# Attention block on one core: units by halves of the sequence, a 512-column output projection, 512-wide value jobs

## What is computed

```
x = x + 0.5 * FFN(layernorm(x))      # FFN: layernorm, ternary 256x256 weight, bias
x = x + ATTN(layernorm(x))           # 16 query heads, 4 key/value heads, head size 128
x = x + 0.5 * FFN(layernorm(x))
# ATTN: q, k, v projections + bias; rotary on q and k; key j is seen by query i
# when 0 <= i - j <= 64; softmax; weights @ v; concatenated heads @ Wo + bo
```

## Time and profile before

| | us |
|---|---|
| median of 3 runs (791.47, 792.79, 792.71) | 792.71 |
| span of the profiled execution, first to last instruction | 790.5 |
| PE busy / PEld busy | 778.3 / 727.2 |
| DVE / ACT / POOL busy | 626.1 / 469.6 / 455.7 |
| mean granted clock of PE, share of full | 0.998 |

### The profile page before, as it was taken

How to read it: one execution, slowest core, us unless ns; L and a number is a source line. 1 busy time by engine, 2 the same in 40 slices (tenths; PEclk the granted TensorE clock), 3 DMA queues, 4 the chain that set the end, 5 groups by cost and what they waited for, 6 DMA issues and landing times.

```text
span 790.5 us, 16087 instructions
## 1 busy us (share of the span) xinstructions
PE 778.3 (98%) x5630; PEld 727.2 (92%) x5630; DVE 626.1 (79%) x1321; ACT 469.6 (59%) x1602; POOL 455.7 (58%) x466
## 2 busy tenths in 40 slices
PE   8999999999999999999999999999999999999997
PEld 7688999999999999999999999999999999999996
DVE  5888967988688877888769887688867988688757
ACT  5366665657646565655747556475664657645574
POOL 3778555766446754567536773476635676446443
PEclk9999999999999999999999999999999999999999
DMA  8572324352252423425153242533224452243410
GB/s 300 114 194 59 90 55 120 95 127 48 55 152 63 121 54 89 126 55 120 41 135 94 68 99 49 134 92 97 67 55 121 94 129 45 57 104 68 107 29 27
DMA packets 54352, 74.10 MB, mean 94 GB/s; under 512 B 7168, under 2 KB 30208, under 8 KB 54272
## 3 DMA queue, kind: packets, MB, share of 16 engines
q1 hardware_dynamic: 53712, 72.74, 37.7%
q10 hardware_dynamic: 560, 0.34, 0.2%
HBM read 14.33 MB, written 4.19 MB: 23 GB/s over the span
## 4 chain that ended last, share of the span: by engine, by line
PE 92%; DVE 3%; POOL 2%; DMA 1%; issue 1%; ACT 0%; SPq 0%; DVEq 0%; POOLq 0%
PE job_p L656 33%; PE attn_p L656 22%; PE scores_p L673 13%; PE heads_p L656 11%; PE probsT_p L737 7%; PE job_p L833 4%; PE job_p L817 2%; POOL q_s L1282 1%; DMA x_res<-wo 1%; POOL probs L1271 1%; DMA x_in<-x 0%; DVE parts L1015 0%; DMA rope_swap<-rope_sin 0%; POOL wo_s L1253 0%; DVE rope_sin L934 0%
## 5 line engine op out<-in xcount | busy, mean ns | idle before, releaser
L656 PE MATMUL attn_p<-wo_s,headsT 128*128 128x256 f32 x1536 | 209.2, 286 | 1.0 <-ACT headsT L1175 0.7
L656 PE MATMUL job_p<-xnT,wq_s 128*128 128x512 f32 x768 | 205.3, 403 | 1.2 <-DVE v_s L951 1.1
L656 PEld LDWEIGHTS attn_p<-wo_s,headsT 128*128 128x128 f32 x1536 | 196.5, 191 | 7.0 <-ACT headsT L1175 1.4
L1154 ACT ACTIVATE probs<-scores_p,neg_max 128x96 f32<-128x96 f32 x512 | 167.6, 352 | 51.8 <-DVE neg_max L900 51.6
L1271 POOL TENSOR_TENSOR probs<-probs,inv_sum 128x384 f32<-128x384 f32 x128 | 107.9, 843 | 152.0 <-DVE inv_sum L906 151.9
L1282 POOL TENSOR_TENSOR q_s<-q_s,rope_swap 128x512 f32<-128x512 f32 x128 | 164.3, 1291 | 52.3 <-DMA rope_swap<-rope_sin 52.2
L1175 ACT ACTIVATE headsT<-heads_p,columns_s 128x512 fp32r<-128x512 f32 x128 | 88.0, 688 | 140.9 <-PE heads_p L656 140.5
L656 PEld LDWEIGHTS job_p<-xnT,wq_s 128*128 128x128 f32 x768 | 135.8, 189 | 26.6 <-DVE v_s L951 1.7
L934 DVE SCALAR_TENSOR_TENSOR rope_sin<-job_p,columns_s,rope_t 128x512 f32<-128x512 f32 x160 | 118.9, 743 | 21.1 <-PE job_p L656 19.9
L673 PE MATMUL scores_p<-k_s,q_s 128*128 128x96 f32 (+2 forms) x1024 | 131.6, 272 | 0.3 <-POOL q_s L1282 0.2
L673 PEld LDWEIGHTS scores_p<-k_s,q_s 128*128 128x128 f32 x1024 | 126.5, 192 | 3.4 <-POOL q_s L1282 1.1
(11 more groups left out here) (96 smaller groups left out, 972.7 us busy)
## 6 DMA issues: line engine op xcount, KB each, us to landing
rope_swap<-rope_sin SPq DMA_DIRECT2D x320, 128.0 KB, 2.3
v_odd<-v_s SPq DMA_DIRECT2D x64, 192.0 KB, 3.3
x_in<-x SPq DMA_DIRECT2D x15, 256.0 KB, 4.2
out<-x_res SPq DMA_DIRECT2D x15, 256.0 KB, 2.5
x_tr<-x_transposed SPq DMA_DIRECT2D x7, 512.0 KB, 5.3
q_s<-wq SPq DMA_DIRECT2D x3, 512.0 KB, 10.1
q_s<-wo SPq DMA_DIRECT2D x2, 512.0 KB, 10.6
x_res<-wo SPq DMA_DIRECT2D x2, 512.0 KB, 4.8
```

Of the source, the lines that this page charges most:

```text
L656: mm = nc.tensor.matmul(dst, a(p), b(q), start=clears and i == 0, stop=len(pairs) == 1, skip_group_check=True)
L1154: ins = nc.scalar.activation(probs[:, i, k, 0:REACH], scores_p[i][:, k, 0:REACH], ACT.Exp, bias=neg_max[:, i, k:k + 1], accum_out=row_sum[ ...
```

## The change

1. `group_block`: units run by halves of the sequence. Units 0 to 7 are groups 0 to 3 with blocks 0 and 1, units 8 to 15 groups 0 to 3 with blocks 2 and 3 (last batch: the last four units by block, groups 2 and 3). A group's `q_s`, `k_s` are free after unit 8 + 2g + 1 (`freed`).
2. `project`: `attn_p` is one tile of two banks; the bank is that of block t % 2, in strips of 256 columns. For each head one matmul of 512 columns (high heads x [high | low] Wo) writes both strips, and one of 256 columns (low x high) adds to strip 0: eight matmuls for twelve, except in the last two units of the last batch.
3. `after_attention` adds both strips: two DVE ops where one was, with a semaphore between them. Both halves use the same two banks.
4. `value_job`: one block of 128 tokens, all 512 value columns: six matmuls of 512 columns; still four jobs a batch. `shift_values`: three shifts a batch, two DMAs each.
5. Banks: the 14 jobs between the prologue's and the first T use four banks, the two of `attn_p` beside `job_p`.
6. `residual` on POOL in halves; one more wait in `exp_of`, in `statistics` and a changed one in `scores`.
7. All five lists are rewritten. K and Q: K0 to K2 and Q0 to Q8 of the next batch are made in the current one (before: K0, Q0 to Q3). In the first batch all 20 K and Q jobs come before unit 6's scores (before: three K and eleven Q). The second FFN of half 0 (YT2_0, FO2_0) comes in its own batch.

Core of the diff:

```diff
 def group_block(x):
     i, b = x[1:]
-    if b < BATCHES - 1 or i < UNITS // 2:
-        return divmod(i, BLOCKS)
-    g, t = divmod(i - UNITS // 2, 2) if i < UNITS - NKV else divmod(i - UNITS + NKV, 2)[::-1]
-    return NKV // 2 + g, t if i < UNITS - NKV else t + BLOCKS // 2
+    g, t = divmod(i % (UNITS // 2), 2)
+    if b == BATCHES - 1 and i >= UNITS - NKV:
+        g, t = NKV // 2 + i % 2, (i - UNITS + NKV) // 2
+    return g, t + (BLOCKS // 2 if i >= UNITS // 2 else 0)
+def freed(g):
+    return UNITS // 2 + 2 * (g + 1)
...
+PROLOGUE_JOBS = 6
+EARLY_JOBS = len(numbered(PE_STEPS[:PE_STEPS.index(("T", 0, 0))], *(x[0] for x in JOB_LIST)))
+BANKS = [n % 2 if n < PROLOGUE_JOBS else (n - PROLOGUE_JOBS) % 4 if n < EARLY_JOBS else (n - EARLY_JOBS) % 2
+         for n in range(len(JOBS))]
...
                 for h in range(GROUP):
-                    products(*head(h), LEFT_HIGH, opens and h == 0)
+                    heads, n = head(h)
+                    if last_pair(x):
+                        products(bank[:, 0, :], heads, lambda s: wo_s[:, s, n, :], LEFT_HIGH, g == NKV // 2 and h == 0)
+                    else:
+                        nc.tensor.matmul(bank, heads(0), wo_s[:, :, n, :], start=g == 0 and h == 0, stop=False,
+                                         skip_group_check=True)
                 pe.wait_ge(heads_lo, u + 1)
                 for h in range(GROUP):
-                    mm = products(*head(h), LEFT_LOW)
+                    heads, n = head(h)
+                    mm = products(bank[:, 0, :], heads, lambda s: wo_s[:, s, n, :], LEFT_LOW)
...
+                if m < 3:
+                    add(blocks, attn_p[:, banks, 1, :]).then_inc(attn_added, 1)
+                    dve.wait_ge(attn_added, 2 * b + m + 1)
+                add(blocks, attn_p[:, banks, 0, :]).then_inc(attn_read, 1)
...
 TENSOR "first"
-        K1c Q4c Q5c S0c S1c Q6c V10c T0c Q7c W0c T1c S2c S3c O0c
+        V0c K0c Q0c Q1c Q2c Q3c Q4c K1c Q5c Q6c Q7c S0c Q8c Q9c V1c S1c T0c Q10c K2c W0c Q11c S2c S3c T1c V2c Q12c
+        O0c Q13c W1c S4c T2c O1c K3c W2c S5c T3c Q14c Q15c O2c W3c T4c FO1_0n O3c W4c T5c S6c S7c O4c V3c W5c T6c
 TENSOR "middle", units 6 to 9
-        W5c T6c Q13c S8c O5c FO0n W6c T7c S9c Q14c FO1n O6c W7c T8c Q15c S10c O7c W8c XT0n T9c
+        T6c S8c XT_0n O5c W6c S9c XT_1n V0n T7c O6c W7c K0n O7c Q0n T8c Q1n W8c Q2n S10c T9c O8c V1n
 VECTOR "middle", the same place
+        heads6c XT_1n V0n probsT7c inv9c heads7c K0n evac0c Q0n probsT8c Q1n stats2_0c heads8c Q2n
 TENSOR "last", its end
-        T14c YT0c O13c W14c T15c O14c YT2c W15c FO0c O15c YT3c FO2c FO3c
+        T14c O13c W14c T15c FO2_0c O14c W15c YT3_2c O15c YT3_3c FO3_2c FO3_3c
 GPSIMD "first", its begin
-        w7f probs0c probs1c K1c Q4c Q5c Q6c Q7c probs2c w9f K2c scale0n probs3c w10f
+        w6f w3f pad0f w8f w10f K0c Q0c Q1c Q2c Q3c Q4c w7f K1c Q5c probs0c Q6c Q7c Q8c Q9c probs1c scale1_0n Q10c
```

More of the change, by code:

```diff
@@ L95 @@
+    "epilogue": "",
 }
@@ L216 @@
 PARTS = {"p": -1, "c": 0, "n": 1}
-WAVES = ("YT", "FO", "stats", "scale", "norm", "bias")
 def program(table):
@@ L225, in program @@
         for step in (table[name] if name in table else table["middle"]).split():
-            kind = step[:-1].rstrip("0123456789")
-            index, part = step[len(kind):-1], step[-1]
+            kind, index = step[:-1].split("_") if "_" in step else (step[:-1].rstrip("0123456789"), None)
+            index, part = index or step[len(kind):-1], step[-1]
             at = b + PARTS[part] if part in PARTS else {"i": -1, "f": 0}[part]
@@ L370, in block_kernel @@
         job_p = [psum(f"job_p{i}", [P, SEQ]) for i in range(2)]
-        attn_p = [psum(f"attn_p{i}", [P, 2, E]) for i in range(2)]
+        attn_p = psum("attn_p", [P, 2, 2, E])
         consts_in = sem("consts_in")
@@ L378, in block_kernel @@
         x_loaded = [sem(f"x_loaded{m}") for m in range(2)]
-        out_stored = sem("out_stored")
+        out_stored = [sem(f"out_stored{m}") for m in range(2)]
         staged = [sem(f"staged{i}") for i in range(10)]
@@ L383, in block_kernel @@
         split_lo_pool = sem("split_lo_pool")
-        v_shifted = sem("v_shifted")
+        v_shifted = [sem(f"v_shifted{m}") for m in range(BLOCKS - 1)]
         ones_set = sem("ones_set")
@@ L662, in scores @@
                 if t == 0:
-                    pe.wait_ge(rope_added, ROPED["Q", GROUP * g + GROUP - 1, b] + 1)
+                    pe.wait_ge(rope_added, max([ROPED["K", g, b]] + [ROPED["Q", GROUP * g + h, b] for h in range(GROUP)]) + 1)
                 pe.wait_ge(mask_ready, u + 1)
@@ L754, in wait_for_bank, with wait_for_sums @@
                     pe.wait_ge(ffn_added, FFN_OUT[was] + 1)
+            def wait_for_bank(x):
+                n = JOBS[x]
+                before = [i for i in range(n) if BANKS[i] == BANKS[n]]
+                if before:
+                    wait_for_job(JOB_LIST[before[-1]])
+                elif BANKS[n] > 1:
+                    wait_for_sums(BANKS[n] - 2)
+            def wait_for_sums(i):
+                if i:
+                    pe.wait_ge(gamma_copied, 1)
+                else:
+                    pe.wait_ge(bias_ready, 1)
+                    if FIRST_BIASED:
+                        pe.wait_ge(first_biased, len(FIRST_BIASED))
             def rope_job(x):
@@ L848, in beta_product @@
                 pe.wait_ge(rows_in, 16)
-                nc.tensor.matmul(attn_p[0][:, 0, :], identf[:, :], half_b, start=True, stop=False)
+                nc.tensor.matmul(attn_p[:, 0, 0, :], identf[:, :], half_b, start=True, stop=False)
                 pe.wait_ge(columns_in, 16)
@@ L1013, in statistics @@
                 half = blocks_of(x)
+                before = [i for y, i in NORMED.items() if i < n and blocks_of(y).start < half.stop and half.start < blocks_of(y).stop]
+                if before:
+                    dve.wait_ge(rstd_ready, 2 * before[-1] + 2)
                 for at in range(half.start, half.stop):
```

333 lines of the change are left out of this document (150 added, 183 removed).

## The result

The changed kernel takes 802.89 us (median of four runs, 800.94 to 804.09) against 792.75 for the kernel before (791.47 to 793.4): ratio 1.0132, 95% interval 1.0111 to 1.0152. It is slower by 10 us where 7.4 of gain were forecast. The profiled execution spans 800.2 us, against 790.5.

What follows compares the result with a forecast made beforehand. PE's own sequence was taken as the bound, busy all 660 us from 80 to 740. Merges -5.8, T/S order -1.2, start -1.9, middle stalls +1.5 gave -7.4 us: median 785.3, range 780.5 to 790.5.

Steps and rivals of the forecast that it cites:

- Merges (part 2 and 4): PE's O and V jobs: 696 merges of two 256-column matmuls into one of 512, 0.0083 us each, 5.8 us gained.
- Order of T and S (part 7): PE's list: scores directly ahead of a transposition 49 times instead of 9, 0.03 us each, 1.2 us gained.
- Middle batches: Shorter T-to-W queue distances on PE: 0.25 us lost a batch, 1.5 in six; bounds 0 and 7.
- Rival (4): Middle batches: stalls of about 1.2 us a batch eat all the gain, 792 us; chance 0.05.
- The held op: Middle batches: narrow DVE op held at ports shared with POOL; 1.2 us in full every batch gave the bound of 7.
- Start: Up to unit 6's scores, put at 74.5 us: net 1.9 us gained; bounds 5 gained and 2 lost.
- Rival (2): Start gains nothing or loses 2 us, POOL and DVE bounding until the last rope job; 787.2 to 789; chance 0.12.
- Four banks: Start's early jobs: four banks absorb the 0.1 to 0.3 us each job loses waiting for DVE with two.
- Rival (1): Middle batch: DVE becomes the bound at evac0, adding both strips; slower, 802 us; chance 0.09.
- The end: Last ops are the same chain with the same lengths, PE still the bound: nothing, between -1 and +1.5 us.

Runs made afterwards that it cites:

- experiment 1: Changed kernel with the 696 merged 512-column matmuls of O and V split back into 256-column pairs: 807.17 us, ratio 1.0189 to the kernel before.
- experiment 9: Changed kernel with XT_0, XT_1 and V0 later on PE in middle batches, ACT's and DVE's lists following: 821.71 us, ratio 1.0374 to the kernel before.
- experiment 12: Changed kernel with POOL's 512-wide residual moved behind the next batch's scale step in middle batches: 805.54 us, ratio 1.0159 to the kernel before.
- experiment 10: Changed kernel with the edits of experiments 4, 5, 6 and 7, plus DVE's heads 5 ahead of the second half's statistics: 805.36 us, ratio 1.0139.
- Experiment 5: Changed kernel with the shift DMAs behind Q6 in SP's list, first and middle batches: 801.23 us, ratio 1.0115 to the kernel before.
- experiment 7: Changed kernel with POOL's first-batch FFN steps behind Q15's add, DVE's and PE's FFN steps later accordingly: 806.12 us, ratio 1.0156 to the kernel before.
- experiment 8: As experiment 7, but unit 6's and 7's probabilities and maxima ahead of most of the moved steps: 807.43 us, ratio 1.0184 to the kernel before.
- experiment 6: Changed kernel with split w3 ahead of w6 on POOL at the very start: 802.56 us, ratio 1.0106 to the kernel before.
- experiment 3: Changed kernel with two job banks throughout, not four for the early jobs: 807.38 us, ratio 1.0173 to the kernel before.
- experiment 2: Changed kernel with DVE's adds of the second strip left out, result incomplete: 803.51 us, ratio 1.0133 to the kernel before.
- experiment 4: Changed kernel with heads 5 and probsT 6 first on ACT, O5 ahead of XT_0 on PE, middle batches: 801.55 us, ratio 1.0117 to the kernel before.
- experiment 13: Changed kernel with the edits of experiments 4, 5, 6 and 12 together: 800.64 us, ratio 1.0092 to the kernel before.
- experiment 14: Changed kernel with the edits of experiments 5, 6 and 12 together: 798.45 us, ratio 1.0082 to the kernel before.

## Why the prediction was wrong

**Merges (part 2 and 4): right, and too small.** Forecast 5.8, measured 7.4 to 8.3 in PE's sequence (experiment 1), though only 4.5 in the time. I took 0.232 for a 512 and 0.120 for a 256 from jobs of one form; in the mixed O of the changed kernel the four of 512 take 0.90 (0.225 each) and the four of 256 take 0.47 (0.118), both a little less. The range's upper bound was 9.

**Order of T and S (part 7): it fits.** 1.2 forecast; 9.4 less 7.4 to 8.3 leaves 1.1 to 2.0. No run tests it by itself.

**Middle batches: the step that failed.** The term was "At 1.4 I take 0.25 a batch"; measured are 2.3 a batch, 13.6 us in six where 1.5 stood in the sum. Rival (4) had 1.2 a batch. I counted queue distances between T and W alone. Half of the loss (7.0 us, at S8 and XT_0) is on another chain, that of the next batch's first half (x_mid, statistics, scale, y, XT, V0), which the change lays into a stretch of PE without K or Q jobs, because units by halves need Q15 by unit 6 and K0 to Q8 of the next batch need XT at once. The text said "the added waits are for steps done long before" and never asked what stands between FO1 and V0. The held op was seen and priced (a 1.2 in full every batch, 7 us, was my bound); that it stands in front of this chain in every batch was not. Experiments 9, 12 and 10 show that the chain has no slack in either direction: the transposes' steps later on DVE and ACT cost 3.2 us a batch (19 in six, 4.7 of them by the clock that fell behind the stall), and what is done sooner for one consumer makes another late by about as much. That the stretch without K and Q jobs is the reason is argued from the list and not shown. A quarter of the loss (3.7 us, at W10) is a second thing that the sum did not have: the shift DMAs stood ahead of Q3's swap in SP's list, where I had only counted that they fall from eight to six. Experiment 5 shows that one, and its cure.

**Start: wrong in sign.** 59.0 us from the first V job to unit 6's scores, where 53.2 were expected (74.5 less the 21.3 of the earlier trace rows). From 18.39 to 81.16 POOL is busy for 54.1 us, close to my 52.2, but idle for 8.6, where I gave "two or three" to waits: 2.4 for the input of w3, 4.1 for swapped halves, 1.8 for inverses. That the FFN steps in the queues are the bound there is shown by experiment 7 (5.8 us sooner without them; POOL is the releaser in the changed kernel, but DVE's steps were moved too), and experiment 8 shows that they must be paid for in that order as well. Of the 5.6 us that the start lost more, 1.7 is the half clock from 81.6 to 85.0 behind the wait for POOL's last Q adds, which no term of the sum had. The hold of 2.86 us ahead of V0 costs 2.1 (experiment 6), more than the 0.9 by which V0 is late. Rival (2) had this place and gave it 2 us at most.

**Four banks: right** in kind, about 3 us (experiment 3); without them the start would be worse still.

**Rival (1)** is refuted (experiment 2). It had put the time at 802, and 802.9 came, but on another path: that was luck. **The end** gave 1.2 that I had put at 0.

What stays open: the changed kernel's 10 us are explained as places, and 4 of them were recovered; the 7.0 at S8 and XT_0 moved to other places and did not go away. Whether an order of the same units exists that spreads the K and Q jobs over the chain to V0 was not tried, nor was the value merge on the old order of units.

## What to carry to other kernels

A kernel in which one engine is busy all the time has two terms, what that engine has to do and what covers the others' latency, and an edit that shortens the first can spend the second, as here. So list for each long chain (here FFN result, statistics, scale, normalise, transpose, first job) which long jobs of the bound engine lie beside it before and after, and where none is left, price what the chain can be late by instead of taking it as covered. When one item is moved in lists that are all full, look for the next one behind it before the gain is booked: here seven local cures (experiments 4 to 9 and 12) each took away or shrank the wait that they were aimed at, and only three of them (4, 5 and 6) came out faster, by 1.2 to 2.1 us, which is at the edge of what the intervals tell. And where a stage gets slower behind a new wait, read the granted clock of that short stretch, since the mean of a long window hides it.

## What the runs showed of the hardware

- A DVE op on 2 columns (0.17 us) took 1.07 in every middle batch, and a normalisation of 0.73 took 2.86, each while a POOL op on SBUF ran, and went back to 0.17 and 0.73 when the POOL op was moved (experiments 12 and 6).
- Two 256-column fp32r matmuls in the place of one of 512 cost 0.0107 to 0.0119 us more, over 696 of them (experiment 1).
- Behind waits of PE of 1.6 to 2.0 us the granted clock fell to half for a while: 0.51 from 81.6 to 85.0 us in the changed kernel, 0.51 from 389.1 to 392.5 in experiment 9, there in four of six middle batches with the same wait. It cost 1.7 and 1.1 to 1.2 us, on top of the wait. It does not come each time: five other traces (experiments 4, 6, 12, 13 and 14) have the wait of about 1.6 ahead of unit 6's scores and full clock behind it.
